# Residual and variance moved to the end of a step, keys stacked ahead of the queries' store, keys and queries projected earlier

## The reference

```python
x = _layernorm(x + _L0_attn_ref(x, ...))                       # mixer; it adds x once more itself
x = _layernorm(x + _L0_xattn_ref(x, ctx_1024, ctx_1024, ...))  # attention
x = _layernorm(x + _L0_ffn_ref(x, ...))                        # experts
```

## Time and profile before

| | |
|---|---|
| median of three runs | 976.9 us |
| profiled execution, its own time | 973.87 us |
| its span | 972.1 us |
| PE busy | 805.2 us (83%) |
| DVE busy | 594.3 us (61%) |
| ACT busy | 404.9 us (42%) |
| POOL busy | 356.3 us (37%) |
| a 256 KB load of `x`, issue to landing | 3.8 us |
| a store of a half, issue to landing | 2.5 us |
| a part of `kst` or `qst`, issue to landing | 3.2 us |

### The profile page before, as it was taken

One profiled execution on the slowest core, in us unless ns is written; L12 is line 12 of the kernel. 1 busy time (PEld: TensorE's weight loads), 2 busy tenths in 40 slices (PEclk: granted clock), 3 DMA queues, 4 the chain that ended last, 5 costly groups with the idle time before them and its releaser, 6 DMA issues. The chain is left out here.

```text
span 972.1 us, 16867 instructions
## 1 busy us (share of the span) xinstructions
PE 805.2 (83%) x5933; PEld 635.1 (65%) x5933; DVE 594.3 (61%) x1410; ACT 404.9 (42%) x639; POOL 356.3 (37%) x290
## 2 busy tenths in 40 slices
PE   5999955568998888899888887885299999999993
PEld 4777734345666666666656665543299999999993
DVE  4879854444578776777877766643255555555542
ACT  4565621123555554455455545551243233423320
POOL 0333434212254444455354444223222344235422
PEclk9999988767999999999999999875599999999997
DMA  4116401553554454464455434100533332233100
GB/s 121 44 45 201 131 19 60 127 136 94 125 132 130 114 156 136 125 157 119 115 136 157 130 111 131 55 21 21 177 96 101 115 108 98 91 114 120 38 27 18
DMA packets 75913, 100.91 MB, mean 104 GB/s; under 512 B 10961, under 2 KB 63354, under 8 KB 75856
## 3 DMA queue, kind: packets, MB, share of 16 engines
q1 hardware_dynamic: 72400, 92.03, 34.0%
q0 software_dynamic: 3456, 8.13, 2.3%
HBM read 65.47 MB, written 35.74 MB: 104 GB/s over the span
## 5 line engine op out<-in xcount | busy, mean ns | idle before, releaser
L971 DVE TENSOR_REDUCE nmax<-ps_m 128x4 f32<-128x1024 f32 x128 | 156.7, 1224 | 117.5 <-PE ps_m L732 114.7
L925 ACT ACTIVATE pt<-ps_a 128x1024 f32<-128x1024 f32 x128 | 131.1, 1024 | 138.0 <-PE ps_a L742 136.6
L1238 ACT ACTIVATE hid<-ps_h 128x640 fp32r<-128x640 f32 x64 | 45.1, 705 | 151.3 <-PE ps_h L1178 151.3
L1178 PE MATMUL ps_h<-xt,w_hi 128*128 128x320 f32 x512 | 100.0, 318 | 1.0 <-DVE xt L1253 1.0
L732 PE MATMUL ps_m<-kst,qst 48*128 48x256 f32 x512 | 68.7, 349 | 33.7 <-DMA qst<-halves_dram 30.1
L732 PEld LDWEIGHTS ps_m<-kst,qst 48*128 48x128 f32 x512 | 41.2, 199 | 77.8 <-issue 35.6
L1287 DVE SCALAR_TENSOR_TENSOR hid<-ps_h,hid 128x640 fp32r<-128x640 f32 x64 | 52.8, 825 | 56.1 <-ACT hid L1238 55.6
L1190 PE MATMUL ps_y<-w_hi,hid 128*128 128x256 f32 x640 | 85.3, 284 | 1.7 <-issue 1.7
L1178 PEld LDWEIGHTS ps_h<-xt,w_hi 128*128 128x128 f32 x512 | 80.1, 191 | 5.5 <-DVE hid L1287 3.3
L1190 PEld LDWEIGHTS ps_y<-w_hi,hid 128*128 128x128 f32 x640 | 80.1, 191 | 1.9 <-issue 1.9
L166 POOL TENSOR_TENSOR gated<-xh,sgate 128x512 f32<-128x512 f32 x32 | 42.2, 1319 | 88.1 <-ACT xh L259 88.1
(11 more groups left out here) (169 smaller groups left out, 1623.9 us busy)
## 6 DMA issues: line engine op xcount, KB each, us to landing
halves_dram<-half SPq DMA_DIRECT2D x64, 256.0 KB, 2.5
gated<-in_w SPq DMA_DIRECT2D x16, 1024.0 KB, 5.5
kst<-halves_dram SPq DMA_DIRECT2D x64, 128.0 KB, 3.2
qst<-halves_dram SPq DMA_DIRECT2D x64, 128.0 KB, 3.2
rows_dram<-blank SPq DMA_DIRECT2D x1, 5160.0 KB, 19.2
gated<-rows_dram SPq DMA_DIRECT2D x8, 645.0 KB, 4.2
x_raw<-in_x_t SPq DMA_DIRECT2D x8, 512.0 KB, 3.8
xres<-in_x SPq DMA_DIRECT2D x16, 256.0 KB, 3.8
```

Source lines behind the costliest of these rows:

```text
L925: nc.scalar.activation(pt[:, k % 4].rearrange("p s t q -> p (s t q)"), ps_a[:].rearrange("p s t q -> p (s t q)"), ACT.Exp).then_inc(s["exp ...
L971: nc.vector.tensor_reduce(nmax[:, q, :, :, h // 2].rearrange("p t s -> p s t"), ps_m[:], AX.X, ALU.max, negate=True).then_inc(s["max_done" ...
L1178: mm = pe.matmul(ps_h[:, f % 2, c2, 0:HC], w1[a][:, p, k, f * P:(f + 1) * P], xt[:, b, p, k, c2 * HC:(c2 + 1) * HC], start=(n == 0 and k = ...
L1238: nc.scalar.activation(hid[:, HI, f, :].rearrange("p (c n) -> p c n", c=2), ps_h[:, f % 2, :, 0:HC], ACT.Relu).then_inc(s["hid_hi"], 1)
```

## The change

Five things are done at once.

1. DVE forms `r`, its statistics and `ve` of sequence n+1 in slots 14 and 15 of step n and no longer in slots 0 and 1 of step n+1. `x1` moves from slot 3 to slot 0. POOL's power of `ve` goes to the end of its step.
2. PE projects the first half of the keys of n+1 in slot 15 of step n, the second in slot 1; the transpose of `x1` moves from slot 5 to 3, the queries from 7 to 6, which puts them ahead of `count`. ACT's matching copies move up one or two slots.
3. POOL's `residual` of n+1, two tensor operations on 128x512, moves from the end of the step to ahead of the queries' `split_lo`.
4. DVE's `y` moves from slot 6 to 7, behind `sel` and `carry`.
5. SP no longer waits behind a store; a semaphore counts each half of it, and each stack waits for its own. All keys of a part are loaded together, part 0 ahead of the load of the next context, which itself goes ahead of the queries.

```diff
-            def stack(j, p, lo):
+            def keys_in(j, p, lo):
 
+                sp.wait_ge(s["setup_pool"], 3)
                 need(sp, s["att_mm"], (j - 2) * NP + NP // 2 * (lo + 1))
-                sp.wait_ge(s["setup_pool"], 3)
+                sp.wait_ge(k_st[lo], 16 * j + 16)
...
+            def queries_in(j, p, lo):
+
+                settled(sp)
+                need(sp, s["att_mm"], (j - 2) * NP + NP // 2 * (lo + 1))
+                sp.wait_ge(q_st[lo], 16 * j + 16)
...
-                                 half[:, :, m, :].bitcast(F32)).then_inc(stored, 16)
-                settled(sp)
-                sp.wait_ge(stored, j * 32 + 32)
+                                 half[:, :, m, :].bitcast(F32)).then_inc(stored[m], 16)
...
-                    stack(n - 1, 1 - p, 1)
+                    keys_in(n - 1, 1 - p, 1)
+                    queries_in(n - 1, 1 - p, 1)
...
-                    store(n, p, 0, s["k_split"], s["k_stored"])
-                    store(n, p, 1, s["q_split"], s["q_stored"])
-                    stack(n, p, 0)
+                    store(n, p, 0, s["k_split"], k_st)
+                    store(n, p, 1, s["q_split"], q_st)
+                    keys_in(n, p, 0)
                 if on(n, 0) and on(n, -1):
                     load_ctx(n + 1, 1 - p)
+                if on(n, 0):
+                    queries_in(n, p, 0)
...
                     if h == 1 and on(n, 0):
-                        keys(n, p, 0)
+                        keys(n, p, 1)
...
-                    if h == 2 and on(n, 0):
-                        keys(n, p, 1)
-                    if h == 4 and on(n, 4):
-                        router(n - 4)
-                    if h == 5 and on(n, 0):
+                    if h == 3 and on(n, 0):
                         pe.wait_ge(s["k_out"], n + 1)
                         pe.wait_ge(s["x1_done"], n + 1)
                         turn(ps_d, x1, s["x1t_mm"])
+                    if h == 4 and on(n, 4):
+                        router(n - 4)
+                    if h == 6 and on(n, 0):
+                        queries(n, 0)
+                        queries(n, 1)
                     if h == 7 and on(n, 4):
                         count(n - 4)
-                    if h == 7 and on(n, 0):
-                        queries(n, 0)
-                        queries(n, 1)
...
+                    if h == 15 and on(n, -1):
+                        keys(n + 1, q, 0)
...
-                    if h == 4 and on(n, 0):
-                        split_hi(n, s["k_out"], s["k_hi"], s["q_stored"], 32 * n)
-                    if h == 9 and on(n, 0):
-                        split_hi(n, s["q_out"], s["q_hi"], s["k_stored"], 32 * n + 32)
+                    if h == 3 and on(n, 0):
+                        split_hi(n, s["k_out"], s["k_hi"], q_st, 16 * n)
+                    if h == 8 and on(n, 0):
+                        split_hi(n, s["q_out"], s["q_hi"], k_st, 16 * n + 16)
```

More of the change, by code:

```diff
@@ L637, in step @@
                     op.then_inc(s["out_ready"], 1)
+                if on(n, 0) and on(n, -1):
+                    residual(n + 1, q)
                 if on(n, 0):
@@ L649, in step @@
                         ).then_inc(sent[p], 16)
-                if on(n, 0) and on(n, -1):
-                    residual(n + 1, q)
+                if on(n, -1):
+                    pool.wait_ge(s["var1_ready"], n + 2)
+                    nc.gpsimd.tensor_tensor(ve1[:], ve1[:], power[:], ALU.pow).then_inc(s["rstd1"], 1)
                 if on(n, 3):
@@ L861, in split_hi @@
                 act.wait_ge(out, j + 1)
-                need(act, stored, before)
+                need(act, stored[0], before)
+                need(act, stored[1], before)
                 nc.scalar.copy(half[:, 0], kq[:]).then_inc(hi, 1)
@@ L897, in step @@
                         op.then_inc(s["den_done"], 1)
[L898 removed]
+                    if h == 2 and on(n, 0):
                         act.wait_ge(s["k_mm"], n + 1)
@@ L997, in step @@
                         stats(st3, pay[:, p], s["stats3"])
-                    if h == 3 and on(n, 0):
-                        dve.wait_ge(s["rstd1"], n + 1)
-                        need(dve, s["x1_kept"], n)
-                        for t in range(KT):
-                            op = nc.vector.tensor_scalar(x1[:, t, :], r1[:, t, :], mv1[:, t, 0:1], ve1[:, t:t + 1],
-                                                         ALU.subtract, ALU.mult)
-                        op.then_inc(s["x1_done"], 1)
                     if h == 3 and on(n, 4):
@@ L1033, in step @@
                         nc.vector.tensor_tensor(carry[:], carry[:], hot[:, 0, :], ALU.add).then_inc(s["place_done"], 1)
+                    if h == 7 and on(n, -1):
+                        dve.wait_ge(s_in[q], use(n + 1, 16, q))
+                        need(dve, s["wout_mm"], n + 1)
+                        for m in range(MH):
+                            op = nc.vector.scalar_tensor_tensor(y[:, m, :], sb[:, q], c["d_col"][:, m:m + 1],
+                                                                gated[:, m, bass.ds((n + 1) * S, S)], ALU.add, ALU.mult)
+                        op.then_inc(s["y_done"], 1)
                     if h == 8 and on(n, 4):
@@ L1057, in step @@
                                                 ).then_inc(s["on_done"], 1)
+                    if h == 14 and on(n, -1):
+                        dve.wait_ge(s["wout_mm"], n + 2)
+                        dve.wait_ge(s["x_added"], n + 2)
+                        nc.vector.tensor_tensor(r1[:].rearrange("p t d -> p (t d)"), ps_d[:],
+                                                c["x2b"][:].rearrange("p t d -> p (t d)"), ALU.add
+                                                ).then_inc(s["r1_done"], 1)
+                        dve.wait_ge(s["r1_done"], n + 2)
+                        stats(st1, r1, s["stats1"])
+                    if h == 15 and on(n, -1):
+                        mean_var(dc, st1, mv1, s["stats1"], n + 1)
+                        nc.vector.tensor_scalar(ve1[:], mv1[:, :, 1], EPS, None, ALU.add).then_inc(s["var1_ready"], 1)
                     if h == 15 and on(n, 3):
@@ L1067, in step @@
                         nc.vector.tensor_scalar(ve2[:], mv2[:, :, 1], EPS, None, ALU.add).then_inc(s["var2_ready"], 1)
-                    if h == 6 and on(n, -1):
-                        dve.wait_ge(s_in[q], use(n + 1, 16, q))
-                        need(dve, s["wout_mm"], n + 1)
-                        for m in range(MH):
-                            op = nc.vector.scalar_tensor_tensor(y[:, m, :], sb[:, q], c["d_col"][:, m:m + 1],
-                                                                gated[:, m, bass.ds((n + 1) * S, S)], ALU.add, ALU.mult)
-                        op.then_inc(s["y_done"], 1)
             run(dve, step)
```

41 lines of the change are left out of this document (18 added, 23 removed).

## The result

The changed kernel takes 988.1 us (median of 4 runs, 984.65 to 988.99) beside 975.0 us for the kernel before (4 runs). The ratio is 1.0133, with a 95% interval of 1.0098 to 1.0167: slower. The prediction was 969.5 us and faster, with a range that ended at 985. The profiled execution after took 988.99 us with a span of 987.2.

The account below looks back on a forecast made before the run. It took PE as the bound, with DVE behind it. Early steps -10.2, steady steps +6.6 and step 15 -3.8 made -7.4 us: 969.5 us against a median of 976.9, with an 8-in-10 range of 953 to 985.

Parts of the forecast that it names:

- The early steps: Steps 1 to 3: waits for the stack and `r` go, 10.2 us gained, bounds 3 and 14 us.
- steps 4 to 14: Eleven steady steps: `y` held by POOL's residual and queries' split, +0.6 us a step, +6.6 in all.
- step 15: No `y`, no residual, half the keys: the wait at step 16 and some others go, -3.8 us.
- A full-clock step with `y` held and `pay` free: Steady step in which POOL delays `y` but not `pay`: 28.7 us, for 28.28 recorded.
- With neither held: Steady steps if `y` were not held: PE 1.2 us sooner a step; as a rival, chance 0.11, median 950.
- The early gain: Path: first scores 0.7 us sooner, PE 6 us ahead at step 2's start, 10 after it, 10.2 in all.
- step 3, said to have little left to lose: Last of the early steps: brings the lead only from 10 us to 10.2.
- the forecast's own time line: Step 10 followed through DVE, POOL and PE from slot 14 at 432.16 to the next start at 463.94.
- the sum for DVE in steady steps: Slot 0 reduction, then `x1` (0.65) and `pay` (0.73): `pay` ends at 440.16, was 440.81.
- My rival for `pay`: POOL's kept `x1` makes the second `pay` operation wait 1.2 us in steady steps; median 982.7, chance 0.20.
- The +6.6: Loss over eleven steady steps: 28.7 us a step against about 28.1 at full clock, +0.6 each.
- the forecast's point: Predicted median for the whole kernel, 969.5 us against 976.9 before; chance of this forecast 0.52.

Follow-up runs that it names:

- run 1: Changed kernel with GpSimd's kept x1 made to wait until VectorE's `pay` pair is done: 956.4 us, ratio 0.9809 to before.
- run 4: Changed kernel with the kept x1 behind `pay` and the residual back behind the scatter: 945.5 us, ratio 0.9717 to before.
- run 2: Changed kernel with the kept x1 made by a copy instead of the addition of b_o, nothing moved: 961.3 us.
- run 5: Changed kernel with eight extra transposes on TensorE in the pause ahead of its wait for `pay`: 964.9 us.
- run 3: Changed kernel with GpSimd's residual put back behind the two DMAs of the scatter: 971.6 us.
- run 6: Changed kernel with eight extra transposes on TensorE behind its wait for `pay`, so the pause stays: 983.8 us.
- run 7: Kernel before with only SyncE's queue order changed (keys, next context, queries, a semaphore for each half): 984.4 us.
- run 8: Kernel before with SyncE's new queue order and eight extra transposes in TensorE's wait for `r`, from step 4 on: 967.7 us.
- run 11: Changed kernel with the kept x1 behind `pay`, residual behind the scatter, and extra transposes in three waits outside the steady steps: 944.4 us.

## Why the prediction was wrong

**The sum, term by term.** The early steps gave -8.6 us for -10.2, steps 4 to 14 +27.1 for +6.6, and step 15 -2.3 for -3.8 (24.9 us for 27.2). The middle term is what went wrong.

**What held.** The waits for `r`, `hot` and the stack went. `y` is held by the residual and the split where the clock is full: forecast 3.5 to 4.3 us, measured 3.7 in steps 8 and 10, and in ten steps of run 1. A full-clock step with `y` held and `pay` free: forecast 28.7, 28.5 on average in run 1. With neither held: 28.3 less 1.2, so 27.1 forecast, 27.1 in run 4.

The early gain is right in its sum and not in its path, which is luck in part: steps 1 and 2 gave 6.6 us for the 10 forecast, and step 3, said to have little left to lose, gave another 2.

Step 10 can be laid beside the forecast's own time line, by taking 5.48 us off, so that slot 14 is at 432.16 in both (437.64 after):

| point | forecast | measured | late by |
|---|---|---|---|
| `pay` ends | 440.16 | 441.21 | 1.05 |
| keys' split starts on POOL | 442.1 | 443.14 | 1.0 |
| `twice` ends | 446.8 | 447.9 | 1.1 |
| `y` ends (next reduction) | 451.75 | 452.74 | 1.0 |
| PE's second `sums_by_query` | 454.03 | 455.03 | 1.0 |
| next step starts | 463.94 | 464.88 | 0.9 |

In this step everything behind `pay` is right but for one and the same microsecond. Only steps 8 and 10 went like this; in the others the clock fell.

**The step that failed** is the sum for DVE in steady steps, "`pay`, which ends at 438.78 + 0.65 + 0.73 = 440.16". It took 0.73 from a row in which POOL was still, though the same argument had just been made for `y`. I saw the rival and gave it 0.20, for a poor reason: that the pair takes as long as two statistics over as many elements does not show that it cannot be held. The earlier trace rows spoke the other way, and I set it aside because its scalars are constants. Run 1 shows that the kept x1 holds the pair, and run 2 that a copy does so too, for as long as it runs. The Trainium skill ("SBUF — State Buffer", Who interferes with whom) states that one of the two engines gets the shared ports for a whole instruction when VectorE runs in certain modes, and that `tensor_scalar` can run in them; here the trace agrees with the hold (a pair of 0.73 us takes 1.70 beside an operation of 1.26), though no run shows the mode itself. The rule should have had the greater chance.

**The term that was missing** is the clock, which the sum kept full. My rival for `pay` gave 1.8 us a step and 982.7; the steps came out 2.5 us longer, at 988. From the profiles, over steps 4 to 14: the lower clock 19.8 us (343.4 to 323.6, run 5), the hold of `pay` 10.4 (323.6 to 313.2, runs 5 and 1, the transposes gone too), the hold of `y` 15.3 (313.2 to 297.9, runs 1 and 4). Without the three, the change would have been worth 18.4 us in these steps (316.3 to 297.9) beside its early gain. These are differences between kernels taken in one order; in another order the shares differ, since the clock answers to the holds. Undone alone, the hold of `pay` gives back 30.2 us, clock included (run 1), and the move of the residual 19.1 (343.4 to 324.3, run 3).

**A third error, hidden by the others.** The +6.6 itself was too much. It comes from setting 28.7 us beside the 28.1 of full-clock steps, but the eleven steps before average 28.8, since the clock falls in four of them. With `pay` free they take 3.1 us less than before (313.2 for 316.3, run 1), and that kernel ran at 956.4, 13 us under the forecast's point.

**What stays open** is which pattern of work brings the clock down. Most falls come behind a wait of 1.5 to 2.1 us that follows the start of a step closely (the changed kernel, runs 3, 6 and 7), but not behind every one, and some come elsewhere (12 to 13 us into three steps of run 8). The same wait does less where PE has more to do around it (run 6). Nor is it shown what the 18.4 us are made of: of the five parts of the change only the order of the queue and the early residual were tried alone.

## What to carry to other kernels

When an operation is moved, list for both engines of a pair what will run beside it, and charge VectorE's operations of the kinds that were held here (`tensor_scalar`, `scalar_tensor_tensor`, a small `tensor_tensor`) the rest of GpSimd's operation, whatever the row from a quiet moment says; then order the two with a wait, or by place, where GpSimd can be late. Here that turned a loss of 1.3% into a gain of 2.8%. Watch the granted clock of each step as a term of its own: a change that removes waits may still lower it (run 7, where two short pauses became one; that the joining did it is not shown). Extra work in a pause is a quick test of that, and itself a gain when the clock is what was lost, though not in every wait (run 11).

## What the hardware showed that I had not expected

- Eight useless transposes a step, in a wait of 1.5 us, made the changed kernel 23 us faster (988.1 to 964.9); in a wait of 2.0 us they made another kernel 17 us faster (984.4 to 967.7).
- Removing a wait slowed a kernel: with SyncE's order alone PE lost its waits for the stack and the time rose by 1.0%, the clock in the steps from 0.98 to 0.91.
- A `tensor_scalar` pair with values per partition (0.73 us) ends 0.15 us after the GpSimd operation beside it, be it an addition of 1.26 us or a copy of 0.61. Even the third norm's `ve`, with 2 elements a partition, takes 0.99 us beside the keys' split and 0.17 without.
- Not everything is held. In run 1 the kept `x1` (455.21 to 456.48) lies beside a reduction of the maxima and the statistics, which take their usual 1.22 and 0.74 us. And `twice`, a `tensor_scalar` of POOL's with one tensor input, hardly holds `y`: 1.88 us for 1.66.
